# Value pass of an attention layer: PE waits on one count per group instead of three, and the zero product has 8 columns

## What is computed

```python
Q = (x @ Wq + bq).reshape(n, HEADS, DK)
K = (x @ Wk + bk).reshape(n, HEADS, DK)
V = (x @ Wv + bv).reshape(n, HEADS, DK)
scores = jnp.sum(Q[tgt] * K[src], axis=-1) / math.sqrt(DK)
smax = jax.ops.segment_max(scores, tgt, num_segments=n)
sexp = jnp.exp(scores - smax[tgt])
ssum = jax.ops.segment_sum(sexp, tgt, num_segments=n)
alpha = sexp / (ssum[tgt] + 1e-16)
messages = alpha[:, :, None] * V[src]
agg = jax.ops.segment_sum(messages, tgt, num_segments=n).reshape(n, HID)
```

## Time and profile before

| | us |
|---|---|
| median of 3 runs | 6065.07 |
| lowest and highest run | 6062.72, 6069.36 |
| the profiled execution | 6063.98 |
| its span, from the first instruction to the last | 6062.2 |
| PE busy, DVE busy over the span | 4236.7, 4336.3 |
| ACT busy, POOL busy over the span | 2687.3, 3638.8 |
| the value pass within the span | about 1384 to 1799 |

### The profile page before, as it was taken

One profiled execution on the slowest core, in us unless ns is written; L12 is line 12 of the kernel. 1 busy time (PEld: TensorE's weight loads), 2 busy tenths in 40 slices (PEclk: granted clock), 3 DMA queues, 4 the chain that ended last, 5 costly groups with the idle time before them and its releaser, 6 DMA issues. The chain is left out here.

```text
span 6062.2 us, 111971 instructions
## 1 busy us (share of the span) xinstructions
PE 4236.7 (70%) x22034; PEld 3503.4 (58%) x22035; DVE 4336.3 (72%) x10827; ACT 2687.3 (44%) x6544; POOL 3638.8 (60%) x3882
## 2 busy tenths in 40 slices
PE   2677777748888985777666567777665677667649
PEld 2566666636664555666666456666664566666634
DVE  5887888877665137777777777777777777777754
ACT  0455555535542002555455435545454345545441
POOL 2777777733320007777777477777774777777720
PEclk7888999979998996666676666666666666776759
DMA  3567777744443853333333133333331333333317
GB/s 83 170 205 214 222 208 214 211 128 122 134 140 105 277 165 95 87 87 89 86 92 89 46 85 92 88 85 88 85 92 40 85 80 85 83 81 82 81 26 263
DMA packets 488021, 725.86 MB, mean 120 GB/s; under 512 B 79979, under 2 KB 306626, under 8 KB 487679
## 3 DMA queue, kind: packets, MB, share of 16 engines
q0 software_dynamic: 123968, 282.81, 19.0%
q1 hardware_dynamic: 236544, 350.89, 18.4%
q10 hardware_dynamic: 127166, 88.94, 4.8%
HBM read 601.60 MB, written 120.75 MB: 119 GB/s over the span
## 5 line engine op out<-in xcount | busy, mean ns | idle before, releaser
L1757 POOL DMA_INDIRECT rows<-scratch_gat,index x2496 | 2523.0, 1011 | 1337.9 <-issue 737.6
L2075 PE MATMUL sums<-xr,hot_t 128*128 x5016 | 1032.0, 372 | 258.8 <-DVE z L1995 218.9
L2075 PEld LDWEIGHTS sums<-xr,hot_t 128*128 128x128 f32 x5016 | 915.0, 273 | 314.4 <-issue 297.3
L2130 PE MATMUL sums<-mix,vhot 128*128 128x128 f32 x4992 | 1092.7, 388 | 1.2 <-issue 0.3
L922 POOL DMA_INDIRECT rows<-scratch_kv,index_ring x832 | 841.0, 1011 | 260.7 <-issue 249.3
L2130 PEld LDWEIGHTS sums<-mix,vhot 128*128 128x128 f32 x4992 | 957.3, 285 | 40.2 <-issue 1.1
L1825 ACT ACTIVATE moved_sums<-sums x624 | 372.7, 597 | 1162.7 <-PE sums L2130 1111.3
L1995 DVE TENSOR_TENSOR z<-sums,rows 128x512 f32<-128x512 f32 x624 | 428.5, 687 | 546.0 <-DMA rows<-scratch_gat,index 499.2
L1815 ACT ACTIVATE vhot<-iota,edge_local 128x128 f32<-128x128 f32 x2496 | 788.7, 390 | 0.0
L1357 PE MATMUL sums<-at_hot,lo_hot 128*128 128x200 f32 x2496 | 572.0, 378 | 4.6
L1981 DVE TENSOR_TENSOR mix<-rows,alpha 128x256 f32<-128x256 f32 x1248 | 471.9, 420 | 68.1 <-PE sums L2130 19.8
(11 more groups left out here) (508 smaller groups left out, 5891.1 us busy)
## 6 DMA issues: line engine op xcount, KB each, us to landing
piece<-scratch_adj SPq DMA_DIRECT2D x90, 1280.0 KB, 6.5
local_ring<-scratch_local_rows SPq DMA_DIRECT2D x159, 512.0 KB
scratch_spool<-rows ACTq DMA_DIRECT2D x208, 256.0 KB
vals<-scratch_spool SPq DMA_DIRECT2D x208, 256.0 KB, 2.6
scratch_adj<-stage SPq DMA_DIRECT2D x25, 1600.0 KB
rows<-scratch_gat,index POOLq DMA_INDIRECT x2496
local_ring<-scratch_local_rows ACTq DMA_DIRECT2D x53, 512.0 KB
mask<-scratch_masks SPq DMA_DIRECT2D x234, 80.1 KB
```

What stands on the lines that cost most here:

```text
L1757: eng.indirect_dma_start(rows[:, slot, q, k * LINE:(k + 1) * LINE], None, table, bass.IndirectOffsetOnAxis(ap=index[:, slot, s:s + 1], axis=0)
L2075: ins = eng.matmul(B.ps[:, at + k * D:at + (k + 1) * D], hot_t[:, slot, k * P:(k + 1) * P], queries[:, bass.ds(at_block, D)], start=True, ...
L2130: ins = eng.matmul(B.ps[:, bass.ds(of_block * D, D)], hot[:, v % MIXES, k * P:(k + 1) * P], mix[:, v % MIXES, k * D:(k + 1) * D], start=Fa ...
```

## The change

Three things. PE no longer waits for `halved` and for `mixed`; it waits for `split` alone. GpSimd, ahead of the step that raises the last count of `split`, now waits for DVE's `mixed` of the same group as well as for `halved`, so that this one count stands for the work of DVE, ACT and GpSimd together. And the product of zeros, on which PE's wait hangs, has 8 columns instead of 512.

```diff
@@ gpsimd
                         eng.wait_ge(halved.sem, halved.at(3) + n * 3)
+                        eng.wait_ge(mixed.sem, mixed.at(BODY_GROUPS + 1) + n)
                         eng.tensor_tensor(part(q, 2), rest[:, q, :, 0:extra_width], part(q, 1), ALU.subtract
                                           ).then_inc(split.sem, 1)
@@ tensor
                         n = i * BODY_GROUPS + q
-                        eng.wait_ge(halved.sem, halved.at(2) + n * 3)
                         eng.wait_ge(split.sem, split.at(2) + n * 2)
-                        eng.wait_ge(mixed.sem, mixed.at(BODY_GROUPS + 1) + n)
-                        eng.matmul(B.bank(7), B.zeros[:, 0:P], B.zeros[:, :], start=False, stop=True, skip_group_check=True)
+                        eng.matmul(B.bank(7)[:, 0:8], B.zeros[:, 0:P], B.zeros[:, 0:8], start=False, stop=True, skip_group_check=True)
```

## The result

The kernel before took 6067.22 us (median of 4), the changed one 6029 and 6031 us in the executions that are compared: a ratio of 0.9936, interval 0.9919 to 0.9952. By the ratio that is 39 us less (37 by the medians), where 41 was forecast and 6024 us. One thing must be said beside it, because the ratio leaves it out: of 11 executions of the changed kernel in all, 6 took 6193 to 6207 us; in the one of these that was profiled, PE's clock was at half speed through the whole value pass.

What follows compares the result with a forecast made beforehand. The prediction took PE's own instruction stream, not data, to bound the value pass. Savings of 41.6 + 0 - 0.5 = 41 us from 6065 gave 6024 us, range 6010 to 6042.

Steps and rivals of the forecast that it cites:

- (a): Value pass, PE: two waits fewer save two register instructions, 0.2 us in each of 208 groups, 41.6 us.
- The split in halves: PE's two removed waits: each was taken to cost 0.1 us of sequencer time per group.
- The bound of 27 us: Least saving from the two waits: only the visible 0.13 us gap between groups closes, over 208 groups.
- (b): Zero product of 8 columns for 512 on PE: 0 us taken, bounds 0 and 10 us; frees the array.
- (c): GpSimd's added wait for DVE's product: 0 in the steady state, 0.5 us once at the pass's start.
- The reserve: GpSimd's lead over PE in the value pass, claimed not to be used up: DVE needs 1.32 us a group, PE 1.53.
- Rivals 1 to 3: Nothing won, 0.07; only the open gap closes, 27 us less 0.5, 0.12; both parts add up, 85 us, 0.05.
- Rival 4: PE's clock falls to half in the value pass; with half the groups so, 6146 us; chance 0.04.

## Why the prediction was right, and where it was not

**What bounds the pass.** Right. The sequencer's instruction stream was named as the limit from the earlier trace rows, and the two waits alone gave the whole gain (365.2 us), while two more cost 39.1 us.

**(a) The two waits, 41.6 us.** Measured 41.7 over the pass, a hit so close that luck has a part in it. The 0.2 us was right only as a mean: it was 0.14, 0.20 and 0.19 us in the first three groups of a turn and 0.27 in the fourth with the turn's end, which the forecast had put at 0.2 with its 0.9 us beyond a group left alone (2.63 - 1.74 before, 2.36 - 1.55 after: 0.89 and 0.81). The group inside a turn is 1.54 to 1.61 us, not 1.53. The split in halves was wrong too, 0.125 and 0.075 us, which two equal steps of 0.1 between starts in the earlier trace rows didn't show. The bound of 27 us, a limit by the next weight load, didn't bind: inside a turn the zero load to the next one went from 0.17 to 0.11 us.

**(b) The short product, 0 us.** Right at full clock, by two experiments. The reason given for its worth, that it makes room for (a), was wrong: with 512 columns the pass is 365.2 us. The array's 1.46 us a group from the earlier trace rows had said as much, being below 1.53 with the long product in it.

**(c) GpSimd's wait, 0.5 us once.** Measured 0.7, once, and nothing in the steady state. The reserve did shrink, from 4.1 to 2.7 us, and not for the reason discussed (the last section), but PE never waited for it.

**The sum.** 6024 forecast; 6029 and 6031 in the first four executions and 6020 to 6027 in the later seven, of those at full clock. The range held for these 5; the other 6 of the 11 lie far above it.

**The rivals.** Rivals 1 to 3 fell. Rival 4, the clock, was given 4 in 100, and came in 6 of 11 executions, so the forecast was right in direction and size for 5 of 11 only, and that these are the ones compared is luck. Its price for a group was well worked out, 2.7 us at half clock against 2.59 measured, but it was then laid on half of the groups (6146 us), where all of them had it (6193 to 6207); the step that failed is the one that spoke against it: "PE's busy share of the stretch stays near (368 - 42) / (415 - 42) = 87%, beside 89% now, and the clock was at 0.99 with that". The busy share did stay, 89%, and told nothing of the clock: the same kernel had the other course, where the share read 100% at 0.50, and with five waits it read 83% at 1.00. The forecast had seen the first group run partly at half clock and used it for the array's pace alone; it is there that the two courses part. The only edit that separates the kernels whose clock fell (8 columns everywhere, or none, with one wait or three) from those on the same chip whose clock didn't is the zero product's work in the array. The Trainium skill (TensorE: Matmul & The Clock Gate, "What's actually happening") says that throttled is the default and recent activity releases the clock; that the zero product's work matters the runs bear out, but by the profile PE was busy for 534 of 534 us and the clock stayed at 0.50.

The profiled passes narrow it down further. In all of them the clearing products ahead of the pass ran at half clock, and they differ in whether the clock then rose and stayed up. With 8 columns and one wait it had risen at 1390 us and stayed, or it never rose; without a zero product it never rose; with 8 columns and three waits it rose in the first group and fell behind the first turn's end. With 128 columns, 256, or 512 in the third group it rose out of 3 to 8 us of groups at half clock, and stayed. So where a profiled pass was in its stream of groups at half clock, the clock came up every time with these longer products, and stayed down for over 500 us in the three passes with 8 columns everywhere or none, but for the first group with three waits. Why three waits had the other course in all four executions and one wait in 6 of 11 isn't settled, nor what makes the clock rise ahead of the pass in one execution and not in the next.

## What to carry to other kernels

A wait on a running number cost PE's sequencer 0.075 to 0.125 us here although its count had long been reached, so where the producers idle and the consumer's idle time is called "issue", let one count stand for several and put the extra wait on an engine with slack. A product that computes nothing may still matter: the short one gained nothing at full clock in any run here, and with it the pass ran at half clock in 6 of 11 executions (and in all four with three waits), which cost four times what the waits gave (170.6 against 41.7 us). Left long, or long once per turn, it had full clock in every execution. Look at the granted clock of the stretch and just ahead of it, and at the list of all executions, not at the busy share, before trusting a median.

## What the runs showed of the hardware

GpSimd's small steps became longer without any change of theirs: L2684 from 402 to 696 ns in the median (single-line views, 1400 us to the end of the pass), and GpSimd's busy time in the pass from 138 to 219 us.

```profile
L2684 POOL TENSOR_TENSOR rest<-extra,parts x199: 392/402/406, 1400.8 to 1789.8; 128x36 f32<-128x36 bf16 x199
```

```profile
L2684 POOL TENSOR_TENSOR rest<-extra,parts x200: 401/696/700, 1400.6 to 1751.5; 128x36 f32<-128x36 bf16 x100
```

The first is before, the second after. The timeline of the changed kernel shows where the time goes:

```profile
1599.75 0.74 DVE L2705 TENSOR_TENSOR mix<-vals,extra 128x512 f32<-128x512 f32 x1
1600.71 0.69 DVE L887 TENSOR_TENSOR vhot<-iota,edge_local 128x512 f32<-128x512 f32 x1 [0.21 <-PE sums L2725]
...
1599.91 0.70 POOL L2684 TENSOR_TENSOR rest<-extra,parts 128x36 f32<-128x36 bf16 x1
1601.04 0.47 POOL L2688 TENSOR_TENSOR parts<-rest,parts 128x36 bf16<-128x36 f32 x1 [0.44 <-ACT parts L2671]
...
1604.16 0.26 POOL L2688 TENSOR_TENSOR parts<-rest,parts 128x36 bf16<-128x36 f32 x1 [0.43 <-ACT parts L2675]
```

L2684 ends at 1600.61, 0.12 us after DVE's product (1600.49); L2688 ends at 1601.51, 0.11 us after DVE's next (1601.40); and where DVE stands still, at 1604.16, the same step takes 0.26. So in these rows a GpSimd step that begins beside a DVE instruction with two inputs ends 0.11 to 0.12 us after it. In the changed kernel L2684 begins near the start of one. In the kernel before it begins 0.40 us into L887 (1600.90 beside 1600.50 to 1601.19) and ends at 1601.30, again 0.11 us behind. It goes with the phase and not with the program: in the execution of the changed kernel at half clock the same two steps have medians of 402 and 256 ns, as in the kernel before. The Trainium skill (SBUF — State Buffer, "Terms", the entry on the shared port pair) says that DVE and GpSimd arbitrate for a port pair which one holds for a full instruction while the other is blocked. The trace agrees in part: the steps' ends follow DVE's, but 0.11 us behind it is less than the 0.26 us of such a step alone, so not all of the step waits. It cost nothing here, as GpSimd was two groups ahead, but it is slack that a change in an engine's phase can take.
